# A ViT embedding whose products contract over 48 partitions, and a normalisation that shares its program block

## The reference

```
patches = x cut into 14 x 14 patches of 3*16*16 = 768 numbers each      # all float32
tokens  = patches @ W(768x192) + b;  h = [class_token, tokens] + pos     # 197 tokens an image
y       = (h - mean) / sqrt(var + 1e-5)                                  # over the 192 channels
q       = round(y / s), s = max|y| / 127 over ALL tokens of all images   # "fake quantisation", in bf16 integers
qkv     = q @ round(w_qkv / s_w) ...;  s_q, s_k, s_v = max|.| over everything
```

## Time and profile before

| what | value |
|---|---|
| median of 3 runs | 2128.96 us (2125.84 to 2130.21) |
| the profiled execution's own time | 2127.63 us |
| its span in the trace | 2125.9 us |
| PE busy | 1531.2 us (72%) |
| DVE busy | 1486.6 us (70%) |
| ACT busy | 1361.7 us (64%) |
| POOL busy | 1176.2 us (55%) |

### The profile page before, as it was taken

How to read it: one execution, slowest core, us unless ns; L and a number is a source line. 1 busy time by engine, 2 the same in 40 slices (tenths; PEclk the granted TensorE clock), 3 DMA queues, 4 the chain that set the end, 5 groups by cost and what they waited for, 6 DMA issues and landing times. The chain is left out here.

```text
span 2125.9 us, 51836 instructions
## 1 busy us (share of the span) xinstructions
PE 1531.2 (72%) x12472; PEld 1032.7 (49%) x12473; DVE 1486.6 (70%) x3745; ACT 1361.7 (64%) x3884; POOL 1176.2 (55%) x1918
## 2 busy tenths in 40 slices
PE   1999993785656656555378886888864999993654
PEld 1999992441111111111244443554434988883553
DVE  0555556897777777777556666788876777765996
ACT  0222221543999999999689995777762766663553
POOL 2333330005666666666155554477775888875886
PEclk9999996896555555555555555555556999996776
DMA  5444320001222122122344443544433555553774
GB/s 170 163 163 180 161 89 35 1 0 48 72 85 80 70 83 82 70 80 85 71 130 151 143 144 118 168 152 149 159 121 115 141 138 142 146 164 115 231 230 135
DMA packets 183979, 254.09 MB, mean 120 GB/s; under 512 B 28154, under 2 KB 147243, under 8 KB 180208
## 3 DMA queue, kind: packets, MB, share of 16 engines
q1 hardware_dynamic: 136256, 192.53, 29.3%
q0 software_dynamic: 19840, 39.17, 5.2%
q10 hardware_dynamic: 27808, 21.50, 3.2%
HBM read 140.66 MB, written 107.86 MB: 117 GB/s over the span
## 5 line engine op out<-in xcount | busy, mean ns | idle before, releaser
L984 ACT ACTIVATE exps_summed<-s,neg_shift 128x197 f32<-128x197 f32 x1184 | 482.7, 479 | 34.2 <-POOL neg_shift L851 32.9
L1021 DVE TENSOR_REDUCE score_max<-s 128x788 f32 (+2 forms) x320 | 284.7, 894 | 108.0 <-PE s L925 96.1
L984 ACT ACTIVATION_READ_ACCUMULATOR exps_summed<-s,neg_shift (+1 forms) x1184 | 304.7, 260 | 0.0
L1383 ACT ACTIVATE exps<-st,scalars 128x788 f32<-128x788 f32 (+1 forms) x320 | 246.4, 892 | 16.8 <-PE st L1292 16.8
L2063 POOL DMA_INDIRECT expert_sums<-y_tile,row_places x216 | 216.2, 1001 | 59.5 <-issue 30.3
L380 PE MATMUL mm<-w_tok,x_transposed 128*112 128x192 f32 x1344 | 238.7, 328 | 0.0
L324 ACT COPY x_transposed<-tp 128x672 f32<-128x672 f32 x112 | 80.5, 719 | 238.4 <-PE tp L371 238.4
L357 POOL TENSOR_SCALAR x_patches<-x_tile 112x768 f32<-112x768 f32 x112 | 93.1, 831 | 220.9 <-PE tp L371 181.7
L380 PEld LDWEIGHTS mm<-w_tok,x_transposed 128*112 128x112 f32 x1344 | 214.5, 178 | 0.1
L925 PE MATMUL s<-k_int,qk_int 16*128 16x197 bf16 x768 | 98.7, 355 | 139.0 <-ACT exps_summed L984 126.7
L1203 POOL TENSOR_SCALAR probs<-exps 128x788 bf16<-128x788 f32 (+1 forms) x160 | 130.0, 819 | 102.3 <-ACT exps L1383 102.0
(11 more groups left out here) (416 smaller groups left out, 4569.1 us busy)
## 6 DMA issues: line engine op xcount, KB each, us to landing
x_tile<-in_x SPq DMA_DIRECT2D x24, 1568.0 KB
z_tile<-listed_rows SPq DMA_DIRECT2D x108, 196.0 KB
v_ints<-v_slots SPq DMA_DIRECT2D x32, 480.0 KB, 2.5
v_slots_in<-v_ints SPq DMA_DIRECT2D x32, 480.0 KB, 3.6
q_ints<-qk_int SPq DMA_DIRECT2D x32, 295.5 KB, 2.5
k_ints<-k_int SPq DMA_DIRECT2D x32, 295.5 KB, 2.4
q_shifted<-q_ints SPq DMA_DIRECT2D x32, 295.5 KB, 3.6
k_ones<-k_ints SPq DMA_DIRECT2D x32, 295.5 KB, 4.4
```

The costliest lines, as they stand in the source:

```text
L984: act.activation(gone[:, v % 2, k], ps[v % 3][:, k, 0:SEQ], ACT.Exp, scale=alpha, bias=nb[:, s, to:to + 1], accum_out=p.lsum[:, bass.ds(n ...
L1021: dve.tensor_reduce(columns(m, u), src, op=ALU.max, axis=AXL.X).then_inc(max_done, 1)
L1383: act.activation(ex[:, v % 4, 0:size(u)], src, ACT.Exp, scale=alpha, bias=p.col(C_LNSA)).then_inc(e_ready, 1)
```

## The change

**Products.** A partition now holds one of the 48 rows that a patch has (3 channels x 16 pixel rows), and along it lie the 224 pixels of that row for all 14 patch rows. A product takes one of the 16 pixel columns of a patch: its stationary operand is 48 partitions x 98 tokens, every 32nd number of `x_rows` (every second patch; `h` picks even or odd), its moving one 48 x 192 of `w_tok`. Sixteen products accumulate a token, where there were six. No patch is gathered and nothing is transposed. Image n lies on partitions 0 to 47 and image n + 32 on 64 to 111; their products alternate (`for a in range(2)`) and go to two PSUM banks. `w_tok` is held twice, once for either half. There are 32 pairs of images x 2 halves = 64 steps, each of 32 products.

**Data.** x comes in pieces of one channel of one image, 16 partitions x 14 x 224 numbers, in runs of 896 bytes; four slots of image pairs are loaded ahead, images 0 to 31 on SP's queue, 32 to 63 on ACT's. The class token, positions and the attention's weights come on ACT's queue too. h is stored by two transfers for each pair of images.

**Tokens.** Neighbouring tokens 2p and 2p+1 lie on partition p (98 partitions, `HALF`). `spread` therefore writes every second column of `xq_t`, and the tokens stand there in their own order, so that the outputs in `attend` need one plain operation.

**One block.** `embed` and `normalise` are one block. The maxima and the rounding of the weights move into the last of the eight rounds of `embed`; constants and the class token's statistics move to its start; the ones row of `xq_t` and the bias move to POOL, in pieces; ACT copies the turned weights out, which are now turned in float32.

```diff
-                def load(g, slot):
-                    for ch in range(C_IMG):
-                        sp.dma_start(x_tile[:, slot, ch].rearrange("p r w -> p (r w)"),
-                                     x[bass.ds(g * PB, PB), :, ch, :]).then_inc(x_in[slot], 16)
-                load(0, 0)
-                sp.wait_ge(x_in[0], 48)
-                load(1, 1)
...
-
-                        sp.wait_ge(xs_ready, 28 * i + 14 * s + 14)
-                        if not last:
-                            load(2 * i + 2 + s, s)
...
-                act.dma_start(w_tok[:], I["L0_tok_W"].rearrange("(k f) d -> f k d", f=128)).then_inc(w_in, 16)
...
-                            nc.scalar.copy(xt[:, w % 2, :].rearrange("p (a n) -> p a n", a=2),
-                                           tp[w % 2][:, :, 0:3 * ROWS]).then_inc(xt_ready, 1)
...
-                            pool.tensor_scalar(xs[:, w % 2, :].rearrange("p (f w) -> p f w", w=PATCH), src, 1.0, 0.0,
-                                               ALU.mult, ALU.add).then_inc(xs_ready, 1)
...
-                    for k in range(KCH):
-                        src = xs[:, w % 2, k * 128:(k + 1) * 128]
-                        last = nc.tensor.transpose(tp[w % 2][:, k // 3, (k % 3) * ROWS:(k % 3 + 1) * ROWS],
-                                                   src, p.idf[0:ROWS, 0:ROWS])
-                    last.then_inc(tp_done, 1)
-
...
+    w_tok = p.sb("w_tok", [128, PATCH, D], F32, c)
+    xs = p.sb("x_rows", [128, SLOTS, HW * SIDE], F32, c)
+    mm = [p.ps(f"mm{k}", [128, 2, 512], F32, c) for k in range(2)]
+    bank = p.ps("weight_maxima", [128, 512], F32, c)
...
+    PAIRED = B // 2
+    ROUNDS = PAIRED // SLOTS
...
+    def load(eng, i, s, a):
+
+        b = SLOTS * i + s + a * PAIRED
+        for ch in range(C_IMG):
+            rows = I["x"][bass.ds(b, 1), ch].rearrange("o (hp r) w -> (o r) hp w", r=PATCH)
+            at = 64 * a + PATCH * ch
+            eng.dma_start(xs[at:at + PATCH, s, :].rearrange("p (hp w) -> p hp w", w=HW), rows).then_inc(x_in[s], 16)
+
+    def sync(sp):
+        for s in range(SLOTS):
+            load(sp, 0, s, 0)
+
+        def body(i, last):
+            for s in range(SLOTS):
+                n = SLOTS * i + s
+                sp.wait_ge(mm_done, 2 * n + 2)
+                if not last:
+                    load(sp, i + 1, s, 0)
+                sp.wait_ge(h_ready, 2 * n + 2)
+                for a in range(2):
+                    sp.dma_start(p.hD[bass.ds(n + a * PAIRED, 1), 1:, :].rearrange("o (p h) d -> p (o h) d", p=HALF),
+                                 p.h[:, bass.ds(2 * (n + a * PAIRED), 2), :]).then_inc(h_out, 16)
+        repeat(sp, ROUNDS, body)
+        sp.wait_ge(h_out, 16 * B)
+
+    def scalar(act):
+        for a in range(2):
+            act.dma_start(w_tok[64 * a:64 * a + 48], I["L0_tok_W"].rearrange("(q w) d -> q w d", w=PATCH)).then_inc(w_in, 16)
+        load(act, 0, 0, 1)
...
+        for s in range(1, SLOTS):
+            load(act, 0, s, 1)
+        w = I["L0_attn_w_qkv"]
+        act.dma_start(p.w_rows[:, 0:4, :], w[0:512, :].rearrange("(t o) c -> o t c", o=128)).then_inc(p.qkv_in, 16)
+        act.dma_start(p.w_rows[0:64, 4, :], w[512:576, :]).then_inc(p.qkv_in, 16)
...
+        def body(i, last):
+            for s in range(SLOTS):
+                if not last:
+                    act.wait_ge(mm_done, 2 * (SLOTS * i + s) + 2)
+                    load(act, i + 1, s, 1)
...
+        pe.wait_ge(id_s, 5)
+        pe.wait_ge(w_in, 32)
+
+        def body(i, last):
+            for s in range(SLOTS):
+                pe.wait_ge(x_in[s], 96 * i + 96)
+                for h in range(2):
+                    t = 2 * (SLOTS * i + s) + h
-                    for k in range(KCH):
-                        last = nc.tensor.matmul(mm[w % 2][0:ROWS, 0:D], xt[:, w % 2, k * ROWS:(k + 1) * ROWS],
-                                                w_tok[:, k, :], start=(k == 0), stop=(k == KCH - 1))
-                    last.then_inc(mm_done, 1)
...
-                pe.wait_ge(w_in, 16)
-                transposes(0, 0, 0)
...
-                            dve.tensor_tensor(row, mm[w % 2][0:ROWS, 0:D], posb[:, w, :], ALU.add).then_inc(h_ready, 1)
...
-                            dve.tensor_reduce(p.hmax[:, bass.ds(at, 1)], row, op=ALU.max, axis=AXL.X)
-                            dve.bn_stats(st6[:, w, :], row).then_inc(st_done, 1)
-                            dve.tensor_reduce(p.hmin[:, bass.ds(at, 1)], row, op=ALU.min, axis=AXL.X)
...
+                    for w in range(PATCH):
+                        for a in range(2):
+                            lo = 64 * a
+                            first = PATCH * h + w
+                            last_ins = nc.tensor.matmul(mm[h][0:HALF, a, 0:D],
+                                                        xs[lo:lo + 48, s, first:first + 2 * (HALF - 1) * PATCH + 1:2 * PATCH],
+                                                        w_tok[lo:lo + 48, w, :], start=(w == 0), stop=(w == PATCH - 1))
+                    last_ins.then_inc(mm_done, 1)
+                    if last and (s, h) == (1, 0):
+                        pe.wait_ge(w_max, 1)
+                        turn_maxima(nc, p, bank, p.pm[:, 1:3], 2, p.red)
+                    if last and (s, h) == (1, 1):
+                        pe.wait_ge(w_max, 2)
+                        spread_maxima(nc, p, bank, 2, p.red)
...
+        dve.wait_ge(pos_in, 64)
+        dve.tensor_tensor(posb[:], posb[:], bias[:].rearrange("p (o d) -> p o d", o=1).broadcast_to([HALF, 2, D]), ALU.add).then_inc(pos_s, 1)
+        dve.tensor_tensor(p.cls[:], p.cls[:], crow[:], ALU.add).then_inc(pos_s, 1)
...
+        def body(i, last):
+            for s in range(SLOTS):
+                n = SLOTS * i + s
+                for h in range(2):
+                    t = 2 * n + h
+                    at = bass.ds(t, 1)
+                    row = h4[:, :, at, :].rearrange("p a o d -> p a (o d)")
+                    dve.wait_ge(mm_done, t + 1)
+                    dve.tensor_tensor(row, mm[h][0:HALF, :, 0:D], posb[:, h:h + 1, :].broadcast_to([HALF, 2, D]),
+                                      ALU.add).then_inc(h_ready, 1)
+                    dve.wait_ge(h_ready, t + 1)
...
+                    dve.tensor_reduce(top, row, op=ALU.max, axis=AXL.X)
+                    for a in range(2):
+                        ins = dve.bn_stats(st6[:, h, a, :], row[:, a])
+                    ins.then_inc(st_done, 1)
+                    dve.tensor_reduce(low, row, op=ALU.min, axis=AXL.X)
+                    need(dve, mv_done, t - 1)
+                    need_apart(dve, st_done, t + 1, tick_v)
+                    for a in range(2):
+                        ins = dve.bn_aggr(mv[:, h, a, :], st6[:, h, a, :])
+                    ins.then_inc(ag_done, 1)
+                    dve.wait_ge(ag_done, t + 1)
+                    dve.tensor_copy(mv4[:, :, at, :].rearrange("p a o d -> p a (o d)"), mv[:, h]).then_inc(mv_done, 1)
+                    if last and (s, h) == (0, 1):
+                        weight_maxima()
+                    if last and (s, h) == (1, 0):
+                        dve.wait_ge(p.red, 1)
+                        reduce_maxima(dve, p, bank, 2, link, C_TOP)
+                        dve.sem_inc(w_max, 1)
+                    if last and (s, h) == (1, 1):
+                        weight_integers()
+        repeat(dve, ROUNDS, body)
...
-                sp.dma_start(brow[:], I["L0_attn_b_qkv"].rearrange("(o d) -> o d", o=1)).then_inc(ld, 16)
-                sp.wait_ge(b_in, 1)
-                for j in range(3):
-                    sp.dma_start(cw1[D1 + j:D1 + j + 1, :], bpart[0:1, j, :]).then_inc(b_mv, 16)
...
-                link(dve.memset(x1[D1:KB], 1.0))
...
-                for src, dst, rows, s in ((w_rows[:, 0:4], wq[:, 0:4], 128, C_IW), (w_rows[0:64, 4:5], wq[0:64, 4:5], 64, C_IW),
-                                          (w_tail[:, 0:1], wq[:, 5:6], 128, C_IP), (w_tail[0:64, 1:2], wq[0:64, 6:7], 64, C_IP)):
-                    link(dve.tensor_scalar(src, src, p.col(s, 0, rows), MAGIC, ALU.mult, ALU.add))
-                    link(dve.tensor_scalar(dst, src, MAGIC, None, ALU.subtract))
-                dve.sem_inc(w_ok, 1)
...
-                    g = 2 * i + s
-                    dve.wait_ge(t_done, t + 1)
-                    for dst, src, rows in ((x0, pa[b][:, 0:2, 0:ROWS], 128), (x1, pa[b][0:D1, 2:4, 0:ROWS], D1)):
-                        to = dst[0:rows, bass.ds(g * PB, PB), 1 + 2 * SIDE * w2:1 + 2 * SIDE * (w2 + 1)]
-                        ins = dve.tensor_scalar(to.rearrange("p b (u hp) -> p u b hp", u=2),
-                                                src.rearrange("p u (b hp) -> p u b hp", b=PB), MAGIC, MAGIC, ALU.add, ALU.subtract)
-                    ins.then_inc(x_ready, 1)
...
+    def gpsimd(pool):
+        def ones(g):
+            pool.memset(x1[D1:KB, g * PB:(g + 1) * PB, :], 1.0).then_inc(ones_ok, 1)
+
+        pool.wait_ge(p.mm_done, B)
```

(65 more changed lines are left out.)

683 lines of the change are left out of this document (299 added, 384 removed).

## The result

The changed kernel is slower: 2142.82 us (2140.07 to 2143.40, 5 runs) against 2128.96 us for the kernel before in the same session (2125.84 to 2132.16, 5 runs), a ratio of 1.0063 with a 95% interval of 1.0048 to 1.0078. The forecast was 2120 us.

> The changed kernel once more, so that all of this group have it on the same chip: 1.005 to 1.008 of the kernel before.

What follows compares the result with a forecast made beforehand. PE was taken to bound the embedding, DVE the normalisation's loop. Embedding +23.5, seam -33.3, loop +3 and line 1402 -1 sum to -7.8 us, from 2127.6 to 2120; range 2108 to 2250.

Steps and rivals of the forecast that it cites:

- They hide, barely: Embedding on PE: four weight loads of 98 columns, together 0.29 us, hide behind 0.324 us of streaming if strides cost nothing.
- column step: New embedding: four MATMULs for one pixel column of two images, 0.324 us by streaming, 1024 times, 332 us.
- rival 2: Embedding: strided weight loads bind; 2394 us at twice the time in line, 2242 at three times overlapped; chance 0.10.
- rival 1: Embedding: no concurrency of the two strips in float32; 332 us more, so 2452 us; chance 0.12.
- rival 3: Embedding: MATMULs of the two strips start strictly in order, some 3 ns apart; +6 us, so 2126; chance 0.06.
- rival 4: Embedding: images come too slowly; at 115 GB/s 419 us, +87, so 2207 us; chance 0.04.
- Start: Ahead of the embedding: first product at 20 us, bounds 13 and 30, where PE waited 42.11 us.
- half pace: Start of the embedding: the first MATMULs run at half pace, +2 us.
- Seam: From the embedding's last product to the first rounded piece: 12.5 us, bounds 11 and 18, from 45.8; -33.3 us.
- Bias: Eleven operations on POOL, each under 0.82 us, done about 9 us behind the scales; hides, 0 to 3 us at stake.
- Loop: Normalisation's loop, bound by DVE: 64 pieces of 196 columns instead of 56 of 224, together +3 us.
- Line 1402: Behind the normalisation's loop: 96 DVE operations of 216 ns go; -1 us, bounds -5 and 0.

Runs made afterwards that it cites:

- e1: The changed kernel with 98 neighbouring numbers of x_rows as each product's stationary operand in place of every 32nd: ratio 0.9995 to the kernel before.
- f1: The changed kernel with products of 128 moving columns in place of 192, loads still strided: PE busy 349.6 us in place of 353.3.
- e2: The changed kernel with both images' products on partitions 0 to 47, one strip of rows, loads still strided: 3260 us in total.
- m1: The kernel before, its embedding kept, with the changed kernel's one block and short seam: 2100.22 us against 2131.49, ratio 0.9860.
- e4: The changed kernel with the loop's rounded tokens written to neighbouring columns of xq_t in place of every second one: ratio 1.0074 to the kernel before.
- e3: The changed kernel with both images' products on one strip of rows and neighbouring numbers as stationary operand: 0.319 us from MATMUL to MATMUL.
- e6: The changed kernel with two loops exchanged, sixteen products of one image, then sixteen of the other: 2959.6 us against 2131.5 for the kernel before.
- e5: A run with two strips at work at once; the text does not say which edit carries this label, so no time can be given.
- e7: A run with two strips at work at once, in a session where the kernel before takes 2279 us; the text does not say which edit it is.

## Why the prediction was wrong

Its sign is wrong, and one term makes it so. The step that failed reads: "They hide, barely, if a load that takes every 32nd number (128 bytes apart) goes as fast as one of neighbouring numbers." It does not. The loads take 0.341 us of a column step in place of at most 0.29, and pass the 0.324 of the streaming (e1 and f1 show it). The forecast itself said that above 0.332 its gain is gone. The cause was on the list, as rival 2, at a tenth, and priced at two and three times a load's time, 2242 and 2394 us. If the four loads go in line, as the 0.29 had it, the true price was 0.085 against a bound of 0.074, 1.16 times; if the strips load side by side, it was 0.171, 2.3 times, which lies between the "twice, hidden" and the "three times" of the rival. Which of the two it is, the runs do not show. I had given this rival only large prices and put the rest into the forecast, although the loads filled 90% of the step, so that a price of 1.15 was enough to turn the sign. The slower side was not far away; it was next door.

Point by point:

- *Concurrency (rival 1), right.* Two strips work at once in float32, in the order first, first, second, second. Had it failed, the loss would have been some 1311.6 - 353.3 = 958 us (e2), nearly three times what I priced: the price assumed the full clock, and with one strip at a time the clock did not rise.
- *In order (rival 3).* In the single records of the trace the second strip starts 22 to 25 ns behind the first; it costs nothing, since with neighbouring numbers, where it starts 18 ns behind, a step takes 0.325.
- *Transfers (rival 4), right to exclude.* 139 GB/s, and no wait for them after the first.
- *Start, right:* 20.4 for 20. The half pace until 25.9 us costs 2.6 us (17 pairs of MATMULs start in 5.5 us, which at 0.171 take 2.9) for the 2 of the forecast.
- *Seam, right:* 14.4 for 12.5, within 11 to 18; m1 shows the same with the old embedding.
- *Bias, wrong.* "It hides" at 9 us; it took 13.9. Its three masked operations take 1.8 us each (5.36 for three), where I had allowed at most 0.82. It lies in the stated 0 to 3 us: DVE waits 3.3 us for its first maximum, where it waited 1.5.
- *Loop, mis-sized:* +5.4 for +3. The strided write costs 20 ns an operation, but PE's side hides that (e4); the wait for the bias, 1.8 us more than the wait at that place before, is, by its size, the larger part of the missing 2.4.
- *Line 1402:* in its bounds, not resolved.

The Trainium skill ("SBUF — State Buffer", The DMA port swizzle) has the rule that a line of 16 bytes should be hit at least twice. On weight loads at full clock the runs agree with it: 163 ns at 4 bytes apart, 167 at 8, and 272 at 16. The Trainium skill ("TensorE: Matmul & The Clock Gate", The mechanism) has MATMULs start in program order, without exception. The runs here do not fit that. In the changed kernel's single records the first four MATMULs start at 20.432, 20.439, 20.838 and 20.874 us, while on one strip (e2) the second starts 0.408 us behind the first. So the one that starts 7 ns behind the first must be on the other strip, and that one stands third in program order.

## What to carry to other kernels

Before a change trades wide products for narrow ones on two strips, compare the sum of the weight loads with the streaming; at 0.29 of 0.324 a small price on the loads decides the sign, so price it at 1.1 and 1.2 times first. Keep the float32 numbers of a stationary operand at most 8 bytes apart: 4 and 8 cost the same here, 16 and 128 did not. Do not take a printed clock of 1.00 for granted where the trace has no record yet; compare one instruction that stands in both kernels, as L188 here. And when a change has two parts, cost each alone: here the block's part was worth 1.4% and the products' part took it all back.

## What the runs showed that I had not expected

Work on a single strip left PE at the low clock: 1311.6 us of products on 48 rows without a pause (e2 and e3), and 1166.6 us in e6, with no rise before 1221 us. With two strips at work at once (the changed kernel, e1, e5, e7), and with products over 128 rows (the kernel before), the clock rose within some 6 us of the first MATMUL, or 6.4 in e1. So losing the overlap cost twice in these runs, once in the overlap and once in the clock. What in the work decides it was not tested.

A weight load at a stride of 16 bytes is slower (272 ns) than at 128 (254), and at the low clock the stride of 128 bytes costs nothing. Neither has been explained.
